# The Hadamard products of an FFN's weights, halved on GpSimd and moved among the last projections

## The chip, the cores and the metric

The kernel runs on one core of one Trainium2 chip. The metric is the device time of one execution in microseconds (us).

## The reference

The reference is one transformer block with adaptive layer norm, in float32. Input x is [2, 1024, 256]. From a conditioning vector come shifts, gains and gates for both halves of the block.

```python
h = layernorm(x) * (1 + ca) + sa
x = x + ga * attention(h)          # 16 query heads, 4 key/value heads of 128, causal, projection
h = layernorm(x) * (1 + cb) + sb
x = x + gb * ffn(h)

def ffn(x):                        # HIDDEN 256, INTER 1024
    x = fwht(x * SU_ug) / 64       # normalised Walsh-Hadamard transform
    x_up = x @ W_up.T * (Wscale_ug[:1024] * 64)
    x_gate = x @ W_gate.T * (Wscale_ug[1024:] * 64)
    x = silu(x_gate) * x_up
    x = fwht(x * SU_dp) / 64
    return x @ W_down.T * (Wscale_dp * 64)
```

A Hadamard transform of the activations is linear, so the kernel applies it to the weights instead, once.

## The kernel before

**Products.** A float32 matrix is split into a rounded high part (`_hi`, the type float32r) and a rest (`_lo`). A product is three matmuls: high by high, high by low, low by high (`three`, L1048 to L1050). So every operand of TensorE costs a rounding and a subtraction on other engines.

**Attention.** Eight turns `t` (two batches by four key/value heads). In a turn the eight row tiles `i` of queries are worked in four windows of two tiles, (7,0), (6,1), (5,2), (4,3). A window has nine units (i, j): `T` transposes four heads' probabilities on TensorE (L1177), ScalarE evicts the high part pt_hi (L722), VectorE the rest pt_lo (L946), and two units later `V` multiplies by the values. The transposes go to a ring of two PSUM banks: T of unit n needs pt_lo of unit n-2. `S` are scores; VectorE takes the maximum, ScalarE the exponential, and GpSimd divides by the sum (`normalise`, L573 and L578). `Y` is the projection of a finished row tile, 12 matmuls; VectorE adds it to x (L956). For all this a list, `WALK`, is written out by `walk()`, and each engine goes through it in order and issues its own part. T3 is below the transpose step of unit 3 of the last window of the last turn, V4 the value step of unit 4.

**The weights of the FFN.** They are six pieces of [128, 2, 512]: 0 to 3 are up and gate, 4 and 5 down. Each piece is multiplied by a Hadamard matrix of 256 (the down weights by one of 1024: two butterfly stages `B` on GpSimd, L543 to L549, and the same product). The 256 x 256 matrix is [[H, H], [H, -H]] with H of 128 x 128; in `weights(n)` both halves of the input are multiplied by H or -H and added in PSUM: 2 outputs k x 2 sources x (high, low) = 8 matmuls of 512 columns (L1224, L1225). The order of the pieces is `PIECES = [0, 1, 4, 5, 2, 3]`; n counts in that order. Around a product: `raw_high(n)` rounds the loaded piece (GpSimd, L615; for n = 1 ScalarE, L733), `raw_low(n)` subtracts (VectorE, L965; for n = 0 GpSimd, L621), `weights_high(n)` and `weights_low(n)` scale by SU, round and subtract the result (ScalarE L741, L746; VectorE L974, L979). The rounded input of n has two sets of buffers, in w_hi, w_lo and in o_hi, o_lo; W[n] are the two PSUM banks of its result.

**The FFN's first chunk.** The FFN works on four chunks of 512 rows. For tile m of the inner dimension `G` is gate and up (24 matmuls, `gate_up`), ScalarE makes the Silu (L754), VectorE the product g32 (L989), its rounding g_hi (L992) and the rest g_lo (L994), and `D` multiplies by the down weights (12 matmuls, `down`). In the first chunk these steps are mixed with the pieces (`P`) and the layer norm of the second batch (`L`), in an order written by hand, the list `FIRST`. The later chunks are a loop. D0 is the down step of tile 0, P2 the product n = 2, G0 the gate and up step of tile 0.

Of the kernel before, what the change touches and what calls it, by code (L numbers as in the profile page):

```python
# [73 lines left out]
def walk():  # L74
# [15 lines left out]
    for t in range(TURNS):  # L90
# [16 lines left out]
        for p, pair in enumerate(WINDOWS):  # L107
# [21 lines left out]
            if t + 1 == TURNS and p > 1:  # L129
                fill[2].append((t, "B", p - 2, 0))  # L130
# [13 lines left out]
    return out + [(TURNS - 1, "Y", i, 0) for i in WINDOWS[-1][::-1]]  # L144
# [25 lines left out]
def build(nc, x_in, wqkv, wv, wproj, wmod, c_cols, wug, wdn, su_ug, su_dp, ws_ug, ws_dp, ident_in, mask_in, had_in, out):  # L170
    ctx = ExitStack()
    with ctx:
# [462 lines left out]
        def _(act):  # L635
# [99 lines left out]
            def weights_high(n):  # L735

                piece = PIECES[n]
                for k in range(KH):
                    act.wait_ge(fmm_s, n * KH + k + 1)
                    if piece < 4:  # L740
                        a_.activation(wu_hi[:, k, piece * CH:(piece + 1) * CH], W[n][k], ACT.Identity,  # L741
                                      scale=su_u[:, k:k + 1]).then_inc(fhi_s, 1)
                    else:
                        for one in range(2):
                            m = 2 * (piece - 4) + one
                            last = a_.activation(wd_hi[k][:, m, :], W[n][k][:, one * HID:(one + 1) * HID],  # L746
# [578 lines left out]
```

## Time and profile before

| | us |
|---|---|
| median of 3 runs | 947.99 (946.07 to 948.47) |
| the profiled execution | 945.94 |
| its span in the profile | 944.0 |
| TensorE busy | 921.1 |
| VectorE busy | 641.0 |
| ScalarE busy | 501.2 |
| GpSimd busy | 459.4 |

The rows below are of the one profiled execution; the time that was measured for it is 1.9 us longer than its span, and the median of the runs is 2.05 us above it. Times in the trace count from the start of the span. PE is TensorE, PEld its loading of weights, DVE VectorE, ACT ScalarE, POOL GpSimd, SPq the queue that issues DMAs. The attention takes up the span to about 787 us, the FFN's weights and first chunk to about 840, the other three chunks the rest.

### The profile page before, as it was taken

What the parts mean: (1) busy time and instruction counts of PE and PEld (TensorE: products, weight loads), DVE (VectorE), ACT (ScalarE), POOL (GpSimd) and SP (SyncE); (2) the same over time, 40 slices, a digit from 0 to 9 for tenths busy, and PEclk for the clock granted to TensorE, in tenths of its full rate; (3) what the DMA queues carried; (4) which work ended last, traced back from release to release, by engine and by line L of the source; (5) the groups of instructions that cost most, each with busy time, mean ns of one, the idle gap of its engine ahead of it and who ended that gap; (6) DMA issues with size and microseconds to landing.
All of it is one profiled execution on the core that took longest, in us unless ns stands there. A gap on an engine that the chain in (4) does not pass through costs nothing.

```text
span 944.0 us, 14992 instructions
## 1 busy us (share of the span) xinstructions
PE 921.1 (98%) x5536; PEld 814.0 (86%) x5536; DVE 641.0 (68%) x1312; ACT 501.2 (53%) x1062; POOL 459.4 (49%) x655
## 2 busy tenths in 40 slices
PE   5989999999999999999999999999999999999997
PEld 4878889888888898888888888888888887888886
DVE  6567667865887577647875777478757876864554
ACT  3376556654665466547664766476647665321111
POOL 2375727670767185707671767076717684120000
PEclk9999999999999999999999999999999999999999
DMA  7000100000001000000010000000001011000000
GB/s 278 23 1 1 40 1 23 1 28 1 23 2 40 1 23 1 29 1 23 1 40 1 24 1 30 1 24 1 1 1 46 1 56 46 1 19 5 22 22 22
DMA packets 10179, 21.33 MB, mean 23 GB/s; under 512 B 1280, under 2 KB 5632, under 8 KB 9984
## 3 DMA queue, kind: packets, MB, share of 16 engines
q1 hardware_dynamic: 9392, 20.24, 6.2%
q8 instruction: 41, 0.67, 0.3%
q10 hardware_dynamic: 720, 0.21, 0.1%
q14 instruction: 26, 0.21, 0.1%
HBM read 18.35 MB, written 2.10 MB: 22 GB/s over the span
## 4 chain that ended last, share of the span: by engine, by line
PE 80%; DVE 11%; ACT 6%; issue 2%; DMA 1%; SPq 0%; DVEq 0%; POOL 0%; ACTq 0%
PE ps L1048 18%; PE ps L1050 17%; PE ps L1049 17%; PE ps L1177 10%; PE ps L1166 5%; PE ps L1160 5%; PE ps L1163 5%; DVE ps L942 4%; ACT prob L697 3%; DVE pt_lo L946 2%; ACT pt_hi L722 2%; DVE xhat L820 1%; PE ps L1072 1%; DVE stats L804 1%; DMA w_raw<-in_wqkv 1%
## 5 line engine op out<-in xcount | busy, mean ns | idle before, releaser
L573 POOL TENSOR_TENSOR rinv<-rsum,mone 128x1 f32<-128x1 f32 x256 | 141.4, 552 | 252.9 <-ACT prob L697 252.9
L946 DVE TENSOR_TENSOR pt_lo<-ps,pt_hi 128x512 fp32r<-128x512 f32 x288 | 198.3, 689 | 63.0 <-ACT pt_hi L722 59.9
L722 ACT ACTIVATE pt_hi<-ps 128x512 fp32r<-128x512 f32 x288 | 170.8, 596 | 123.8 <-PE ps L1177 123.5
L697 ACT ACTIVATE prob<-ps,nmax 128x128 f32<-128x128 f32 (+25 forms) x256 | 181.8, 710 | 85.5 <-DVE nmax L942 84.5
L942 DVE CUSTOM_DVE_ANT_0 ps<-ps,mask_f 128x128 f32<-128x128 f32 (+25 forms) x256 | 184.4, 726 | 46.2 <-PE ps L1166 44.1
L578 POOL TENSOR_SCALAR prob<-prob,rinv 128x128 f32<-128x128 f32 (+25 forms) x256 | 187.5, 733 | 43.2 <-POOL rinv L573 43.2
L1177 PE MATMUL ps<-ident,prob 128*128 128x128 f32 x1152 | 172.0, 273 | 1.6 <-POOL prob L578 1.2
L1177 PEld LDWEIGHTS ps<-ident,prob 128*128 128x128 f32 x1152 | 140.5, 140 | 19.9 <-DVE pt_lo L946 2.0
L1048 PE MATMUL ps<-pt_hi,v_hi 128*128 128x512 f32 x288 | 134.2, 466 | 0.0
L1050 PE MATMUL ps<-pt_hi,v_lo 128*128 128x512 f32 x288 | 113.7, 395 | 0.0
L1049 PE MATMUL ps<-pt_lo,v_hi 128*128 128x512 f32 x288 | 113.5, 394 | 0.0
L1160 PE MATMUL ps<-k_hi,q_hi 128*128 128x256 f32 (+16 forms) x384 | 108.3, 336 | 2.7 <-ACT prob L697 2.0
L1166 PE MATMUL ps<-k_hi,q_lo 128*128 128x256 f32 (+16 forms) x384 | 106.7, 332 | 0.0
L1163 PE MATMUL ps<-k_lo,q_hi 128*128 128x256 f32 (+16 forms) x384 | 106.5, 331 | 0.0
L1160 PEld LDWEIGHTS ps<-k_hi,q_hi 128*128 128x128 f32 x384 | 68.8, 189 | 18.3 <-ACT prob L697 7.2
L898 DVE SCALAR_TENSOR_TENSOR q_lo<-ps,q_hi 128x512 fp32r<-128x512 f32 x64 | 44.0, 691 | 53.9 <-ACT q_hi L686 53.9
L686 ACT ACTIVATE q_hi<-ps 128x512 fp32r<-128x512 f32 x64 | 38.3, 599 | 74.5 <-PE ps L1050 74.5
L1163 PEld LDWEIGHTS ps<-k_lo,q_hi 128*128 128x128 f32 x384 | 69.7, 188 | 6.2
L754 ACT ACTIVATE prob<-ps,ws_u 128x512 f32<-128x512 f32 x32 | 22.0, 687 | 97.2 <-PE ps L1050 97.2
L1048 PE MATMUL ps<-wp_hi,o_hi 128*128 128x256 f32 x256 | 73.1, 286 | 0.0
L1166 PEld LDWEIGHTS ps<-k_hi,q_lo 128*128 128x128 f32 x384 | 69.7, 188 | 3.2
L1050 PE MATMUL ps<-wp_hi,o_lo 128*128 128x256 f32 x256 | 72.4, 283 | 0.0
(145 smaller groups left out, 1785.2 us busy)
## 6 DMA issues: line engine op xcount, KB each, us to landing
w_raw<-in_wqkv SPq DMA_DIRECT2D x8, 640.0 KB, 3.9
wp_raw<-in_wproj SPq DMA_DIRECT2D x8, 512.0 KB, 3.4
prob<-in_wug SPq DMA_DIRECT2D x4, 512.0 KB, 5.1
out_y<-prob SPq DMA_DIRECT2D x8, 256.0 KB, 2.2
x<-in_x SPq DMA_DIRECT2D x3, 512.0 KB, 12.7
prob<-in_wmod SPq DMA_DIRECT2D x1, 1024.0 KB, 10.1
wv_raw<-in_wv SPq DMA_DIRECT2D x4, 256.0 KB, 4.9
raw_down<-in_wdn SPq DMA_DIRECT2D x1, 1024.0 KB, 4.7
```

The lines of the kernel that those rows point to most:

```text
L578: g_.tensor_scalar(row(i, h), row(i, h), rinv[:, at, h:h + 1], 1.0, ALU.mult, ALU.mult).then_inc(prob_done, 1)
L697: a_.activation(row(i, h).rearrange("p (a n) -> p a n", a=nb), score_banks(i, h).rearrange("p (a n) -> p a n", a=nb)[:, :, 0:w], ACT.Exp, ...
L722: a_.activation(pt_hi[:, n % 3, :], ring(t, "T", n), ACT.Copy).then_inc(pth_done, 1)
L942: v_.tensor_tensor_reduce(scores, scores, late, -1.0, 3.0e38, ALU.add, ALU.min, nmax[:, place(n), h:h + 1]).then_inc(max_done, 1)
L946: v_.tensor_tensor(pt_lo[:, n % 3, :], ring(t, "T", n), pt_hi[:, n % 3, :].bitcast(F32), ALU.subtract).then_inc(ptl_done, 1)
L1048: mm(dst, w_h, r_h, start=start, stop=False)
L1049: mm(dst, w_h, r_l, start=False, stop=False)
L1050: return mm(dst, w_l, r_h, start=False, stop=stop)
L1160: mm(dst[:, a * CH:a * CH + wide], queries(q_hi, n, h), k_hi[:, a * w:a * w + wide], start=True, stop=False)
L1163: mm(dst[:, a * CH:a * CH + wide], queries(q_hi, n, h), k_lo[:, a * w:a * w + wide], start=False, stop=False)
L1166: last = mm(dst[:, a * CH:a * CH + wide], queries(q_lo, n, h), k_hi[:, a * w:a * w + wide], start=False, stop=True)
L1177: last = tr(ring(t, "T", n)[:, q * P:(q + 1) * P], row(i, q, j * P, (j + 1) * P), ident[:, :])
```

## The change

- The 256-wide product is done as a sum and a difference, H(a + b) and H(a - b), of a piece's two halves. GpSimd forms a + b and a - b for each of the six pieces (`last_butterfly`), two operations of 128x512, and a product is then 2 outputs x (high, low) = 4 matmuls. The matrices -H are gone.
- The butterflies `B` of the down weights stand earlier in `WALK`: the first at the end of window (6,1), which puts it before GpSimd's normalisations of tile 4, the second after the first score step of tile 3.
- The pieces n = 0 and 1 are worked within `WALK`: ScalarE rounds them (`RH`) ahead of its evictions of units 4 and 6 of the last window, GpSimd subtracts, and the products P0 and P1 stand behind the two last projections. n = 1 has the key buffers for its halves and PSUM banks S[1] for its result. Piece 0 is loaded to w_raw, earlier.
- For n = 2 to 5 GpSimd adds, subtracts and rounds, in halves, and VectorE subtracts the low part in halves.
- In the first chunk ScalarE rounds g_hi (`gated_high`) in place of VectorE.

```diff
-            if t + 1 == TURNS and p > 1:
-                fill[2].append((t, "B", p - 2, 0))
+            if t + 1 == TURNS and p in (1, 2):
+                fill[8 if p == 1 else 4].append((t, "B", p - 1, 0))
+            if t + 1 == TURNS and p == 3:
+                for n in range(2):
+                    fill[4 + 2 * n].append((t, "RH", n, 0))
...
-    return out + [(TURNS - 1, "Y", i, 0) for i in WINDOWS[-1][::-1]]
+    for n, i in enumerate(WINDOWS[-1][::-1]):
+        out += [(TURNS - 1, "Y", i, 0), (TURNS - 1, "P", n, 0)]
+    return out
...
-FIRST = [("P", 0), ("P", 1), ("G", 0), ("P", 2), ("G", 1), ("D", 0), ("P", 3), ("G", 2), ("D", 1), ("P", 4), ("G", 3),
+FIRST = [("G", 0), ("P", 2), ("G", 1), ("D", 0), ("P", 3), ("G", 2), ("D", 1), ("P", 4), ("G", 3),
...
+        def halves_of(piece):
+            return raw_sum[sum_slot(piece)], raw[piece][:, 1, :]
...
-        W = [X if n == 1 else T for n in range(len(PIECES))]
+        W = [[S[1][:, 0:CH], S[1][:, CH:2 * CH]] if n == 1 else T for n in range(len(PIECES))]
...
             sp.dma_start(raw_down[:, :], wdn).then_inc(raw_s[4], 16)
+            sp.dma_start(raw[0], wug[0, :, :].rearrange("p (k n) -> p k n", k=KH)).then_inc(raw_s[0], 16)
...
-            for n in range(4):
+            for n in range(1, 4):
...
+            def last_butterfly(n):
+                a, b = raw[n][:, 0, :], raw[n][:, 1, :]
+                pool.wait_ge(fly_s, 2)
+                if n < 4:
+                    pool.wait_ge(raw_s[n], 16)
+                g_.tensor_tensor(raw_sum[sum_slot(n)], a, b, ALU.add)
+                g_.tensor_tensor(b, a, b, ALU.subtract).then_inc(last_fly_s, 1)
...
-            pool.wait_ge(raw_s[0], 16)
-            raw_high(0)
-            pool.wait_ge(rhi_s, 1)
-            g_.tensor_tensor(raw_lo[0], raw[0], raw_hi[0].bitcast(F32), ALU.subtract).then_inc(rlo0_s, 1)
-            pool.wait_ge(fly_s, 2)
+            for n in range(2):
+                last_butterfly(PIECES[n])
+            for n in range(2):
+                pool.wait_ge(rhi_s, n + 1)
+                for k, z in enumerate(halves_of(PIECES[n])):
+                    last = g_.tensor_tensor(raw_lo[n][:, k, :], z, raw_hi[n][:, k, :].bitcast(F32), ALU.subtract)
+                last.then_inc(rlo01_s, 1)
             for n in range(2, len(PIECES)):
-                if PIECES[n] < 4:
-                    pool.wait_ge(raw_s[PIECES[n]], 16)
-                raw_high(n)
+                last_butterfly(PIECES[n])
+                pool.wait_ge(fmm_s, (n - 1) * KH)
+                if n == 3:
+                    pool.wait_ge(y_done, (TURNS + 1) * NT)
+                pool.wait_ge(last_fly_s, n + 1)
+                for k, z in enumerate(halves_of(PIECES[n])):
+                    last = g_.tensor_scalar(raw_hi[n][:, k, :], z, 1.0, 1.0, ALU.mult, ALU.mult)
+                last.then_inc(rhi_s, 1)
...
+                if what == "RH":
+                    act.wait_ge(last_fly_s, n + 1)
+                    if n == 1:
+                        act.wait_ge(s_done, this(s_done, t, 32))
+                    for k, z in enumerate(halves_of(PIECES[n])):
+                        last = a_.activation(raw_hi[n][:, k, :], z, ACT.Copy)
+                    last.then_inc(rhi_s, 1)
+                if what == "P":
+                    weights_high(n)
...
-            act.wait_ge(raw_s[1], 16)
-            act.wait_ge(y_done, (TURNS + 1) * NT)
-            a_.activation(raw_hi[1], raw[1], ACT.Copy).then_inc(rhi1_s, 1)
...
+            def gated_high(m):
+                act.wait_ge(g32_s, m + 3)
+                a_.activation(g_hi[:, g_slot(m), :], g32[:, m % 2, :], ACT.Copy).then_inc(ghi_s, 1)
...
                 if what == "G":
                     gate(0, n)
+                    gated_high(n)
...
+                if what == "P":
+                    weights_low(n)
+                    if n == 1:
+                        raw_low(2)
...
-                gated(0, n)
+                gated(0, n, False)
...
-                plus, minus = mats[:, 0:P], mats[:, P:2 * P]
-                for k in range(KH):
-                    for src in (0, 1):
-                        mat = minus if k and src else plus
-                        mm(W[n][k], mat, raw_hi[n % 2][:, src, :], start=not src, stop=False)
-                        last = mm(W[n][k], mat, raw_lo[n % 2][:, src, :], start=False, stop=bool(src))
-                    last.then_inc(fmm_s, 1)
+                mat = had_r[PIECES[n] // 4]
+                for k in range(KH):
+                    mm(W[n][k], mat, raw_hi[n][:, k, :], start=True, stop=False)
+                    mm(W[n][k], mat, raw_lo[n][:, k, :], start=False, stop=True).then_inc(fmm_s, 1)
...
+                    if n == 1:
+                        pe.wait_ge(wf_ok, KH * 2)
```

## Rows read from the trace of the kernel before

**Rows 1.** The page: busy time of the engines, and the chain by engine.

```profile
PE 921.1 (98%) x5536; PEld 814.0 (86%) x5536; DVE 641.0 (68%) x1312; ACT 501.2 (53%) x1062; POOL 459.4 (49%) x655
...
PE 80%; DVE 11%; ACT 6%; issue 2%; DMA 1%; SPq 0%; DVEq 0%; POOL 0%; ACTq 0%
```

**Rows 2.** Busy time by stretches: engines, granted clock, DMA share, GB/s.

```profile
787.50:798.00 10.50, 9.87 (x53) 7.95 (x52) 6.71 (x9) 5.79 (x8) 2.36 (x2) 1.00 0.22 81
798.00:823.00 25.00, 24.94 (x134) 21.32 (x134) 20.61 (x42) 9.56 (x17) 3.83 (x4) 1.00 0.00 1
```

**Rows 3.** Timeline of TensorE: start, duration, line, out<-in, count, idle before.

```profile
777.61 0.60 PE L1177 MATMUL ps<-ident,prob 128*128 128x128 f32 x4
...
782.43 0.60 PE L1177 MATMUL ps<-ident,prob 128*128 128x128 f32 x4
...
787.50 0.29 PE L1048 MATMUL ps<-wp_hi,o_hi 128*128 128x256 f32 x1
...
790.62 0.40 PE L1224 MATMUL ps<-w_hi,had_r 128*128 128x512 f32 x1
790.85 0.40 PE L1225 MATMUL ps<-w_lo,had_r 128*128 128x512 f32 x1
...
793.25 0.50 PE L1224 MATMUL ps<-o_hi,had_r 128*128 128x512 f32 x1 [0.63 <-DVE o_lo L965]
...
795.21 0.40 PE L1048 MATMUL ps<-h_hi,q_hi 128*128 128x512 f32 x1
...
798.16 0.47 PE L1224 MATMUL ps<-w_hi,had_r 128*128 128x512 f32 x1
...
820.93 0.38 PE L1048 MATMUL ps<-k_hi,pt_hi 128*128 128x256 f32 x1
```

**Rows 4.** Timeline of GpSimd.

```profile
745.59 0.88 POOL L578 TENSOR_SCALAR prob<-prob,rinv 128x736 f32<-128x736 f32 x1 [0.21 <-POOL rinv L573]
...
755.60 1.28 POOL L512 TENSOR_TENSOR h_lo<-h,h_hi 128x512 fp32r<-128x512 f32 x1
...
764.41 2.40 POOL L543 TENSOR_TENSOR sum_down<-raw_down 128x1024 f32<-128x1024 f32 x1
...
769.12 0.55 POOL L573 TENSOR_TENSOR rinv<-rsum,mone 128x1 f32<-128x1 f32 x1
...
776.40 1.29 POOL L548 TENSOR_TENSOR raw_down<-sum_down 128x512 f32<-128x512 f32 x1
...
781.41 1.05 POOL L615 TENSOR_SCALAR w_hi<-prob 128x1024 fp32r<-128x1024 f32 x1
...
800.41 1.36 POOL L615 TENSOR_SCALAR w_hi<-prob 128x1024 fp32r<-128x1024 f32 x1 [3.91 <-PE ps L1225]
```

**Rows 5.** Timeline of the DMA queue SP.

```profile
772.27 0.33 SPq L478 DMA_DIRECT2D prob<-in_had  x1
```

**Rows 6.** Timeline of ScalarE.

```profile
716.64 1.16 ACT L672 ACTIVATE v_hi<-raw_down 128x512 fp32r<-128x512 f32 x2
...
780.79 0.60 ACT L722 ACTIVATE pt_hi<-ps 128x512 fp32r<-128x512 f32 x1 [1.96 <-PE ps L1177]
...
788.32 1.28 ACT L730 ACT_TABLE_LOAD   x1
```

**Rows 7.** Timeline of VectorE in the first chunk.

```profile
799.71 0.43 DVE L992 CAST pt_hi<-prob 128x512 fp32r<-128x512 f32 x1
800.17 0.69 DVE L994 TENSOR_TENSOR pt_lo<-prob,pt_hi 128x512 fp32r<-128x512 f32 x1
...
814.80 0.75 DVE L804 BATCH_NORM_STATS2 stats<-x 128x6 f32<-128x256 f32 x2
...
818.95 0.74 DVE L989 SCALAR_TENSOR_TENSOR prob<-ps,ws_u,prob 128x512 f32<-128x512 f32 x1
```

**Rows 8.** Timeline of VectorE: the same pair of operations at two times.

```profile
745.89 1.05 DVE L820 TENSOR_SCALAR xhat<-x,mv,rstd 128x256 f32<-128x256 f32 x2
...
817.04 0.73 DVE L820 TENSOR_SCALAR xhat<-x,mv,rstd 128x256 f32<-128x256 f32 x2 [0.90 <-POOL rstd L505]
```

More of the change, by code:

```diff
@@ L242, in build @@
         guard_a, guard_b = sum_dn[:, 0, :, :], sum_dn[:, 1, :, :]
-        had_f = prob[:, 0, 0, 0:CH].rearrange("p (a n) -> p a n", a=2)
-        raw = [prob[:, n // 2, n % 2 * 2:n % 2 * 2 + 2, CH:2 * CH] for n in range(4)]
+        had_f = prob[:, 0, 0, 0:2 * P].rearrange("p (a n) -> p a n", a=2)
+        raw = [w_raw[:, :, 0:CH] if n == 0 else prob[:, n // 2, n % 2 * 2:n % 2 * 2 + 2, CH:2 * CH] for n in range(4)]
         raw += [raw_down[:, n * KH * CH:(n + 1) * KH * CH].rearrange("p (k n) -> p k n", k=KH) for n in range(2)]
@@ L686, in chunk, with weights_high @@
                     a_.activation(query_chunk(q_hi, h, half), by_squares(bank(t, c)), ACT.Copy, scale=SCALE).then_inc(qkv_hi, 1)
+            def weights_high(n):
+                piece = PIECES[n]
+                for k in range(KH):
+                    act.wait_ge(fmm_s, n * KH + k + 1)
+                    if piece < 4:
+                        a_.activation(wu_hi[:, k, piece * CH:(piece + 1) * CH], W[n][k], ACT.Identity,
+                                      scale=su_u[:, k:k + 1]).then_inc(fhi_s, 1)
+                    else:
+                        for one in range(2):
+                            m = 2 * (piece - 4) + one
+                            last = a_.activation(wd_hi[k][:, m, :], W[n][k][:, one * HID:(one + 1) * HID],
+                                                 ACT.Identity, scale=su_d[:, 4 * k + m:4 * k + m + 1])
+                        last.then_inc(fhi_s, 1)
             waiting = []
@@ L730, in _ @@
             a_.activation(sc[:, 1, :, :], sc[:, 0, :, :], ACT.Silu)
-            act.wait_ge(raw_s[1], 16)
-            act.wait_ge(y_done, (TURNS + 1) * NT)
-            a_.activation(raw_hi[1], raw[1], ACT.Copy).then_inc(rhi1_s, 1)
-            def weights_high(n):
-                piece = PIECES[n]
-                for k in range(KH):
[L739 to L746, printed above, removed]
-                                                 ACT.Identity, scale=su_d[:, 4 * k + m:4 * k + m + 1])
-                        last.then_inc(fhi_s, 1)
             def gate(c, m):
@@ L905, in v_low, with raw_low, weights_low @@
                                      v_hi[:, 4 * n:4 * n + 4, :].bitcast(F32), ALU.subtract).then_inc(v_lo_s, 1)
+            def raw_low(n):
+                dve.wait_ge(rhi_s, n + 1)
+                for k, z in enumerate(halves_of(PIECES[n])):
+                    last = v_.tensor_tensor(raw_lo[n][:, k, :], z, raw_hi[n][:, k, :].bitcast(F32), ALU.subtract)
+                last.then_inc(rlo_s, 1)
+            def weights_low(n):
+                piece = PIECES[n]
+                for k in range(KH):
+                    dve.wait_ge(fhi_s, n * KH + k + 1)
+                    if piece < 4:
+                        at = slice(piece * CH, (piece + 1) * CH)
+                        v_.scalar_tensor_tensor(wu_lo[:, k, at], W[n][k], su_u[:, k:k + 1], wu_hi[:, k, at].bitcast(F32),
+                                                ALU.mult, ALU.subtract).then_inc(wf_ok, 1)
+                    else:
+                        for one in range(2):
+                            m = 2 * (piece - 4) + one
+                            last = v_.scalar_tensor_tensor(wd_lo[k][:, m, :], W[n][k][:, one * HID:(one + 1) * HID],
+                                                           su_d[:, 4 * k + m:4 * k + m + 1], wd_hi[k][:, m, :].bitcast(F32),
+                                                           ALU.mult, ALU.subtract)
+                        last.then_inc(wf_ok, 1)
             for t, what, n, h in WALK:
@@ L991, in gated @@
                 dve.wait_ge(g32_s, c * NM + m + 3)
[L992 removed]
+                if split:
+                    v_.tensor_copy(g_hi[:, g_slot(m), :], g32[:, m % 2, :]).then_inc(ghi_s, 1)
                 dve.wait_ge(ghi_s, c * NM + m + 1)
@@ L1132, in chunk, with weights @@
                 last.then_inc(qkv_done, 1)
+            def weights(n):
+                if n == 0:
+                    pe.wait_ge(ptl_done, (TURNS + 1) * NU)
+                    pe.wait_ge(consts, 1)
+                if n == 1:
+                    pe.wait_ge(exp_done, this(exp_done, TURNS - 1, 32))
+                if n < 2:
+                    pe.wait_ge(rlo01_s, n + 1)
+                else:
+                    pe.wait_ge(rlo_s, n - 1)
+                    pe.wait_ge(wf_ok, KH * n)
+                mat = had_r[PIECES[n] // 4]
+                for k in range(KH):
+                    mm(W[n][k], mat, raw_hi[n][:, k, :], start=True, stop=False)
+                    mm(W[n][k], mat, raw_lo[n][:, k, :], start=False, stop=True).then_inc(fmm_s, 1)
             for t, what, n, h in WALK:
@@ L1303 @@
         had = np.block([[had, had], [had, -had]])
-    had = np.concatenate([s * had / n ** 0.5 for n in (HID, INTER) for s in (1, -1)], axis=1).astype(np.float32)
+    had = np.concatenate([had / n ** 0.5 for n in (HID, INTER)], axis=1).astype(np.float32)
     arrays = {
```

57 lines of the change are left out of this document (13 added, 44 removed).

## The prediction

> **What bounds the kernel now.** I read the page first: TensorE is busy 98% of the span, and the chain that ended last lies 80% on it [rows 1]. Anything else matters only where it makes TensorE wait or work. The table of stretches then shows the place of the change, the hand-over from the last attention window to the FFN: TensorE is busy 9.87 of 10.50 us there and 24.94 of 25.00 in the stretch behind, at a granted clock of 1.00 (the level of 2.4 GHz) [rows 2]. So two things can be won: matmuls, and some 0.6 us of idle time. In the matmul timeline [rows 3] see the order of the steps named above: T3 777.61, T6 782.43, first Y 787.50, P0 790.62, P1 793.25, G0 795.21, P2 798.16, D3 820.93. The one start with idle time printed is P1: 0.63 us, for a VectorE subtraction.
>
> **Less TensorE work.** The 512-column matmuls of a piece start 0.23 us apart [rows 3]. A piece has 8 of them before and 4 after: six pieces save 24 x 0.232 = 5.6 us of TensorE time. If TensorE stayed the only limit, that and the idle time would be the whole gain. The sums and differences go to GpSimd, and all that follows is about who becomes late instead.
>
> **GpSimd and the last window.** The second butterfly stage is four operations of 128x512, from 776.40 to 781.41 [rows 4]: 1.25 us each, so a piece's sum and difference cost 2.5 us. GpSimd works in program order, and both stages move ahead: the first (764.41 to 769.12, 4.7 us) now stands before the four normalisations of row tile 4, the second (5.0) before the last three of tile 3. A normalisation costs 1.46 (five from 769.12 to 776.40 [rows 4]). From the end of h_lo at 755.60 + 1.28 = 756.9: stage one to 761.6, five normalisations to 768.9, stage two to 773.9, three more to 778.3. Before, the last was done at 776.4. The transposes T3 start at 777.61 [rows 3], the fourth needs the last normalisation 0.33 later: T3 stalls about 0.4 us.
> Then the first pair runs 778.3 to 780.85, the second to 783.4 (the DMA of its raw piece is the first behind the load issued at 772.27 [rows 5], so in time; the other raw piece comes before the window). ScalarE's rounding of piece 0 stands in front of its eviction of unit 4, which began at 780.79 [rows 6]. ScalarE is in order, so this eviction, VectorE's pt_lo and V4 queue behind GpSimd. Two 128x512 copies from SBUF take 1.16 us [rows 6]: 780.9 to 782.0, eviction (0.60) to 782.65, pt_lo (0.69, the form of g_lo [rows 7]) to 783.4. T6 needs that buffer and was at 782.43: +1.0. Rounding piece 1 waits for the second pair: 783.4 to 784.6, eviction of unit 6 and pt_lo to 785.95; T8, two units of 1.13 behind T6, was at 784.69: +1.3. The last window ends 1.3 us later; the 0.4 of T3 is inside that.
> GpSimd then makes the low halves of pieces 0 and 1, to 786.0 and 788.5 (2 x 1.25 each), before P0 and P1 need them (790 and 792). The copies of the Hadamard matrices halve, which VectorE's waits hide.
>
> **The hand-over.** The first Y starts at 787.50 + 1.3 = 788.8. Y 1.44 (12 matmuls of 0.12), P0 0.93 (4 x 0.232), Y 1.44, P1 0.93 put G0 at 793.55, against 795.21: -1.65. P0 fills the time in which the second Y waited, and P1's halves are ready. The Silu table load (1.28 [rows 6]) moves behind the evictions of P1, to about 794.6 to 795.9; G0's first Silu can begin at 796.5, which hides it by 0.6 us.
>
> **From G0 to D3: VectorE and ScalarE.** TensorE's own work there is 5 G x 2.73 + 4 P x 0.93 + 3 D x 1.44 = 21.7 us; before it was 25.72 (820.93 - 795.21), with P at 1.86. But VectorE's chain was nearly full: its g32 of tile 3 began only at 818.95, behind a layer norm begun at 814.80 [rows 7], and D3 waited for it. What the change does to that chain: the cast of g_hi (0.43, next start 0.46 later [rows 7]) goes to ScalarE, but VectorE is in order and waits for it, and one copy of 128x512 there is 0.60 to 0.64 with the hand-over (half of 1.16, and the fill [rows 6]): +0.18 each. And ScalarE now rounds g before it evicts the piece behind it. A round with a down piece: g32 0.79, wait 0.64, g_lo 0.60, wait for the piece's first eviction 0.24, two subtractions 0.79, 0.12 more of waiting, 0.79, raw_low in two halves 1.21: 5.18 us. With an up piece 4.66. So G0's start + 2.73 + 0.26 + 0.72 (Silu) = 3.7; two rounds 10.35; one of 4.66; layer norm 4.15 (814.80 to 818.95); the last round up to g_lo 2.2. Together 25.1 us against 25.7: only 0.6 of the 3.7 us saved on P2 to P5 survive. It shows as idle time of TensorE: about 1 us before D0, about 2 before D3. I add 0.3 for small gaps that such a sum leaves out. Without anything else D3 is 1.65 + 0.6 - 0.3 = 2.0 us earlier. Behind D3 a G, D and L take 4.6 us and VectorE 4 to 4.5, and the later chunks are untouched: the shift stays.
>
> **Contention, the unknown term.** The rows show GpSimd and VectorE holding each other up when both work from SBUF. VectorE's two xhat that began 0.3 us inside a GpSimd scaling of 0.88 us took 1.05 against 0.73 alone [rows 4, 8]; GpSimd's rounding that began inside VectorE's g_lo of 800.17 took 1.36 against 1.05 [rows 4, 7]. After the change GpSimd is busy about 90% of the time from 788.5 to 804 (four times 2.5 + 1.2), and in that time VectorE has six subtractions with both inputs in SBUF (raw_low of pieces 4 and 5 in halves, g_lo of tiles 0 and 1), all on its full chain. Lower bound: nothing. Upper bound: each waits for a whole sum, 1.0 us, 6 us in all. Between them: an op that comes at a random point waits some 0.6 less the 0.2 that the xhat row shows to be free before the end, times six, some 2.4; a part falls into VectorE's waits for ScalarE (0.36 a round). I take 1.3.
> The Trainium skill (SBUF — State Buffer, Who interferes with whom) says that a VectorE instruction with two SBUF inputs contends with a GpSimd one that reads SBUF, and that the loser blocks until the other is through. The xhat and rounding rows agree in direction; that it holds for a VectorE subtraction behind a GpSimd sum no row here shows. What it gives is rival 2.
>
> **Sum.** Profiled execution: 945.94 (span 944.0 and 1.9 around it) - 2.0 + 1.3 = 945.2. The median of the runs is 947.99, 2.05 above the profiled one; the same difference gives 947.3, a gain of 0.07%. A measurement of this kernel tells about 0.3% (2.8 us) from no change.
>
> **Rivals.**
> 1. TensorE keeps its saving. If ScalarE and VectorE had slack that I don't see, the gain is 5.6 + 0.9 of idle time - 1.3 (last window) = 5.2: 942.8. Against it: D3 already waited for VectorE. The partial form (no contention, and no stall in the last window because GpSimd is through sooner) is 2.0 + 1.3 = 3.3: 944.7. Chance of a gain over 2.8: 0.15.
> 2. Slower: VectorE held by GpSimd. If the six subtractions wait a full 1.0 us each and the two casts of the Hadamard matrices, in front of pt_lo of unit 5, 0.5 each, the term is 7 and the result -2.0 + 7 = +5: 953. It decides from a mean wait of 0.8 us on (six times 0.8 = 4.8, less 2.0). GpSimd's sums back to back speak for it; that the xhat pair lost only 0.3 speaks against. Chance 0.13.
> 3. No contention on the path: -2.0, 946.0. Chance 0.22, inside "same".
> 4. My case, 947.3, between 946.3 and 950.5: 0.50.
>
> **How the numbers follow.** Cases 3 and 4 are "same", 0.72; faster 0.15; slower 0.13. The range goes from the partial form of rival 1 (944.9) to a contention term of 4.6 (950.6).
>
> **What would show it.** Right: four matmuls a piece; T3, T6 and T8 late by 0.4, 1.0, 1.3; G0 at 793.5; idle time of 1 us before D0 and of 2 us before D3, both released by VectorE; raw_low and g_lo longer than 0.69 us while GpSimd adds. Wrong: D3 without idle time (rival 1), subtractions of 1.5 us and more (rival 2), or the transposes of units 4 to 8 on their old spacing of 1.13 us.

## The result, and the profile after

| us | before | after |
|---|---|---|
| median of 18 runs each, on the same chips | 946.21 (945.85 to 948.48) | 948.33 (946.49 to 951.06) |
| the profiled execution | 945.94 | 950.35 |
| its span | 944.0 | 948.4 |

The ratio of the times is 1.0018, with a 95% interval of 1.001 to 1.0025: slower by about 1.7 us, where a gain of 0.07% was forecast. The times of each kernel lie on levels some 2 us apart, so medians and means differ: the medians stand 2.1 us apart, the means (946.75 and 948.53) 1.8. The loss is 1.7 to 2.1 us.

The 18 runs of after don't scatter evenly. Each has its mean granted clock beside it:

| runs of after | us | mean granted clock |
|---|---|---|
| 6 | 946.49 to 947.42 | 0.998 to 0.999 |
| 7 | 948.10 to 949.53 | 0.998 |
| 5, the profiled one among them | 950.20 to 951.06 | 0.994 |

That turns out to be half of the story.

First the page of after, its busy times and its chain by engine, against [rows 1]:

```profile
PE 920.6 (97%) x5512; PEld 813.0 (86%) x5512; DVE 640.4 (68%) x1307; ACT 506.4 (53%) x1073; POOL 478.8 (50%) x673
...
PE 74%; DVE 13%; ACT 6%; POOL 3%; issue 2%; DMA 0%; DVEq 0%; SPq 0%; POOLq 0%; ACTq 0%
```

The 24 matmuls are gone (5536 to 5512), but TensorE is busy only 0.5 us less, not 5.6. Its share of the chain fell from 80 to 74%, and GpSimd, absent before, holds 3%. So 5.1 us of matmul time came back (the two falls of the clock below are in it), and TensorE's idle time grew by 4.9 us, from 22.9 to 27.8 of the span. Now the stretches, with the columns of [rows 2]; the first is early in the attention, the last four follow each other behind it:

```profile
48.00:60.00 12.00, 9.55 (x39) 7.66 (x38) 6.69 (x18) 7.07 (x20) 8.99 (x14) 0.73 0.01 2
787.50:798.00 10.50, 10.48 (x61) 8.81 (x61) 6.79 (x12) 5.87 (x9) 9.18 (x10) 1.00 0.30 100
798.00:823.00 25.00, 20.86 (x105) 16.68 (x103) 20.53 (x37) 9.93 (x21) 11.94 (x12) 1.00 0.01 1
822.00:824.00 2.00, 0.17 (x1) 0.18 (x2) 1.23 (x3) 1.65 (x3) 0.44 (x1) 1.00 0.00 0
824.00:826.00 2.00, 2.00 (x14) 2.00 (x15) 1.75 (x3) 0.93 (x3) 0.00 (x0) 0.71 0.00 0
826.00:828.00 2.00, 2.00 (x8) 1.71 (x7) 1.39 (x4) 1.44 (x3) 0.00 (x0) 0.50 0.06 12
828.00:830.00 2.00, 2.00 (x10) 1.60 (x9) 1.59 (x6) 0.00 (x0) 1.45 (x2) 0.93 0.00 0
```

Three things stand here. In the first chunk (798 to 823) TensorE is idle for 4.1 of 25 us, which was 0.06. GpSimd works 9.18 of the 10.5 us of the hand-over, which was 2.36. And the granted clock falls twice. It is 0.73 in 48 to 60, long before anything that the change touches (1.00 in the profile of before). That fall comes in single executions of both kernels: of 33 runs of before beside experiment 1, four have a mean clock of 0.996 and lie at 948.14 to 948.63, some 2 us above the others' middle of 946.4. No trace of such a run of before was taken, but of the thirteen profiles here seven show the early fall (0.72 to 0.86 in 48 to 60 us), and all seven are of executions on the upper level of their kernel (948.61 against 946.2 to 946.6 in experiment 1, 945.97 against 944.2 to 944.6 in experiment 3); the other six show 1.00. In after's profile the clock falls again to 0.50, the level of 1.2 GHz, right after TensorE was nearly idle (0.17 of 2.00 us). That one belongs to the change.

Because of that early fall I compare by marks inside the last window, in us from its first transposes. T, Y, G, P, D and L are the steps named above; L1, the layer norm step behind D4, is the mark for what follows D3 (D3, L0, G5, D4, L1).

| | T6 | T8 | Y | G0 | P2 | D0 | P3 | D3 | L1 |
|---|---|---|---|---|---|---|---|---|---|
| before | 9.66 | 11.92 | 14.73 | 22.44 | 25.39 | 30.04 | 31.48 | 48.16 | 54.32 |
| after | 10.45 | 13.68 | 16.50 | 21.21 | 24.75 | 29.85 | 32.82 | 49.00 | 56.74 |
| after minus before | +0.79 | +1.76 | +1.77 | -1.23 | -0.64 | -0.19 | +1.34 | +0.84 | +2.42 |

G0 is 1.2 us sooner; by D3 that and 0.8 more are gone; between D3 and L1 another 1.6. The timeline of TensorE shows where it stood (columns of [rows 3]):

```profile
785.28 0.66 PE L1232 MATMUL ps<-ident,prob 128*128 128x128 f32 x4 [0.20 <-DVE pt_lo L1011]
...
787.31 0.66 PE L1232 MATMUL ps<-ident,prob 128*128 128x128 f32 x4 [0.68 <-DVE pt_lo L1011]
...
799.58 0.50 PE L1186 MATMUL ps<-w_hi,had_r 128*128 128x512 f32 x1 [0.66 <-DVE w_lo L948]
...
804.68 0.39 PE L1086 MATMUL ps<-k_hi,pt_hi 128*128 128x256 f32 x1 [1.14 <-DVE v_lo L963]
...
807.65 0.50 PE L1186 MATMUL ps<-o_hi,had_r 128*128 128x512 f32 x1 [1.29 <-DVE o_lo L948]
...
823.83 0.38 PE L1086 MATMUL ps<-k_hi,pt_hi 128*128 128x256 f32 x1 [1.87 <-DVE pt_lo L1032]
```

The two T rows are T6 and T7. P2, D0, P3 and D3 wait 0.66, 1.14, 1.29 and 1.87 us, together 5.0, each for a VectorE instruction. D0 and D3 were forecast (1 and 2 us); P2 and P3 were not. VectorE in that stretch, against [rows 7]:

```profile
785.14 1.52 DVE L984 CAST had_r<-prob 128x128 fp32r<-128x128 f32 x2
...
797.82 0.68 DVE L948 TENSOR_TENSOR w_lo<-sum_down,w_hi 128x512 fp32r<-128x512 f32 x1
798.42 1.10 DVE L948 TENSOR_TENSOR w_lo<-raw_down,w_hi 128x512 fp32r<-128x512 f32 x1
...
801.26 1.80 DVE L1032 TENSOR_TENSOR pt_lo<-prob,pt_hi 128x512 fp32r<-128x512 f32 x1 [0.77 <-ACT pt_hi L791]
...
804.55 1.36 DVE L948 TENSOR_TENSOR o_lo<-sum_down,o_hi 128x512 fp32r<-128x512 f32 x1
805.84 1.76 DVE L948 TENSOR_TENSOR o_lo<-raw_down,o_hi 128x512 fp32r<-128x512 f32 x1
...
809.03 1.07 DVE L1032 TENSOR_TENSOR pt_lo<-prob,pt_hi 128x512 fp32r<-128x512 f32 x1 [0.77 <-ACT pt_hi L791]
...
823.08 0.69 DVE L1032 TENSOR_TENSOR pt_lo<-prob,pt_hi 128x512 fp32r<-128x512 f32 x1 [0.77 <-ACT pt_hi L791]
```

And GpSimd, in the form of [rows 4], with the last normalisations left out:

```profile
780.28 1.30 POOL L575 TENSOR_TENSOR dif_down<-w_raw 128x512 f32<-128x512 f32 x1
...
797.85 1.13 POOL L651 TENSOR_SCALAR o_hi<-sum_down 128x512 fp32r<-128x512 f32 x1 [0.19 <-POOL raw_down L576]
798.95 1.05 POOL L651 TENSOR_SCALAR o_hi<-raw_down 128x512 fp32r<-128x512 f32 x1
799.97 1.29 POOL L575 TENSOR_TENSOR dif_down<-prob 128x512 f32<-128x512 f32 x1
801.23 1.28 POOL L576 TENSOR_TENSOR prob<-prob 128x512 f32<-128x512 f32 x1
...
804.09 1.28 POOL L575 TENSOR_TENSOR dif_down<-prob 128x512 f32<-128x512 f32 x1
805.33 1.73 POOL L576 TENSOR_TENSOR prob<-prob 128x512 f32<-128x512 f32 x1
808.94 0.62 POOL L651 TENSOR_SCALAR o_hi<-dif_down 128x512 fp32r<-128x512 f32 x1 [1.89 <-PE ps L1187]
```

Put the two side by side. g_lo of tile 0 begins at 801.26, 0.03 us inside the GpSimd difference of 801.23. That ends at 802.51, g_lo at 803.06: it takes 1.80 where the same form takes 0.69 at 823.08, with GpSimd quiet. The same sum for all five that are stretched:

| VectorE subtraction begins | GpSimd instruction that it meets ends | subtraction ends | behind it by |
|---|---|---|---|
| 798.42 | 797.85 + 1.13 = 798.98 | 799.52 | 0.54 |
| 801.26 | 801.23 + 1.28 = 802.51 | 803.06 | 0.55 |
| 804.55 | 804.09 + 1.28 = 805.37 | 805.91 | 0.54 |
| 805.84 | 805.33 + 1.73 = 807.06 | 807.60 | 0.54 |
| 809.03 | 808.94 + 0.62 = 809.56 | 810.10 | 0.54 |

Whatever the meeting, a sum or a rounding, early in it or late, the subtraction ends 0.54 us behind the other's end. It doesn't run slower, it stands: of its 0.68 us only 0.14 pass beside the other. The same holds in all the traces of the experiments: 39 subtractions of this form that begin inside a GpSimd instruction, in eleven kernels, end 0.52 to 0.56 us behind it. Over 0.68 alone the five lose 0.42 + 1.12 + 0.68 + 1.08 + 0.39 = 3.7 us. It goes both ways: the GpSimd difference of 805.33 met the o_lo of 804.55, and took 1.73 against 1.28. The two casts of the Hadamard matrices, in front of the pt_lo that T7 waits for, take 1.52 together at 785.14, beside GpSimd's difference of piece 1 and low half of piece 0.

### The profile page after: what moved, and what is told of

The parts are those of the page before. It is cut to its first block, busy times and chain, and to the rows that moved or that the text cites. A ratio compares the mean times of both kernels' runs of the same rounds, so it can differ in the third digit from the quotient of the medians.

```text
span 948.4 us, 14983 instructions
## 1 busy us (share of the span) xinstructions
PE 920.6 (97%) x5512; PEld 813.0 (86%) x5512; DVE 640.4 (68%) x1307; ACT 506.4 (53%) x1073; POOL 478.8 (50%) x673
## 2 busy tenths in 40 slices
DMA packets 10180, 21.21 MB, mean 22 GB/s; under 512 B 1280, under 2 KB 5760, under 8 KB 9984
## 4 chain that ended last, share of the span: by engine, by line
PE 74%; DVE 13%; ACT 6%; POOL 3%; issue 2%; DMA 0%; DVEq 0%; SPq 0%; POOLq 0%; ACTq 0%
PE ps L1086 17%; PE ps L1088 16%; PE ps L1087 16%; PE ps L1232 9%; PE ps L1215 5%; PE ps L1218 5%; PE ps L1221 5%; DVE ps L1007 4%; ACT prob L738 3%; DVE pt_lo L1011 2%; ACT pt_hi L763 2%; DVE xhat L857 1%; PE ps L1110 1%; DVE stats L841 1%; POOL prob L604 1%
## 5 line engine op out<-in xcount | busy, mean ns | idle before, releaser
L1087 PE MATMUL ps<-wp_lo,o_hi 128*128 128x256 f32 x256 | 72.1, 282 | 0.0
```

Source lines behind the costliest of these rows:

```text
L1087: mm(dst, w_h, r_l, start=False, stop=False)
```

## The experiments

Times are medians, with the ratio to runs of before taken beside them, and its 95% interval. After stands at 948.33, ratio 1.0018.

**1. g_hi back to VectorE.** After, without the part that gives the rounding to ScalarE:

```diff
-                    gated_high(n)
...
-                    gated(0, n, False)
+                    gated(0, n)
```

> The changed kernel, but VectorE rounds g_hi in the first chunk again. In the changed kernel's trace the way from g32's start to g_lo's start is 1.51 us (before: 1.25), four times ahead of D3, and ScalarE's evictions of the down pieces wait behind the rounding. Theory 'the hop to ScalarE is a main cost': D3 comes 1.0 to 1.5 us sooner after G0 (27.8 us now), median down by 1 us or more. Rival 'VectorE is held by GpSimd': the cast is one more VectorE operation from SBUF, is itself held by GpSimd in tiles 0 and 1, and D3 gains under 0.5 us.

Measured: 946.55, ratio 1.0002 (0.9993 to 1.0011). D3 is at 48.20, 0.8 sooner than after, less than the 1.0 to 1.5 expected: in tile 0 the cast on VectorE is itself held by GpSimd (1.01 us in place of 0.43). In the idle time before it, and in the clock behind it, the profile differs too:

```profile
823.65 0.38 PE L1085 MATMUL ps<-k_hi,pt_hi 128*128 128x256 f32 x1 [1.15 <-DVE pt_lo L1031]
```

```profile
824.00:826.00 2.00, 2.00 (x18) 1.96 (x17) 1.97 (x4) 0.12 (x1) 0.00 (x0) 1.00 0.00 0
826.00:828.00 2.00, 2.00 (x11) 1.64 (x10) 1.97 (x6) 0.90 (x2) 0.17 (x1) 1.00 0.03 8
```

1.15 us of idle time instead of 1.87, and the clock stays at 1.00 (2.4 GHz). Of the 1.5 us (by the ratios) to 1.8 us (by the medians) recovered, 0.8 is the position of D3; the rest is this, as I read it. The hop to ScalarE costs the chain 0.27 a tile, since g_lo starts 1.52 us after g32 begins (799.74 to 801.26) where it was 1.25 (798.92 to 800.17); I had 0.18.

**2. More matmuls in the idle time.** After, with the first six matmuls of G4, the G in front of D3, done twice (1.37 us more work):

```diff
-                for a in (0, 1):
+                for a in ((0, 0, 1) if twice else (0, 1)):
...
-                    gate_up(0, n)
+                    gate_up(0, n, n == 4)
```

> The changed kernel, with the first six matmuls of G4 done twice (1.37 us more TensorE work, inside the 2.5 us in which TensorE waits for D3's input; the result is the same). Theory 'the granted clock falls after the idle time before D3 and costs 1.6 us': the clock stays at 1.00 from 824 to 830 in the trace, D3 to L1 takes 6.2 us instead of 7.7, the median falls by 0.8 to 1.6 and the spread of the runs shrinks. Rival 'all of the loss is waiting, the fall of the clock is harmless or independent of this idle time': no change in time.

Measured: 947.1, and all 11 runs lie within 946.97 to 947.23; ratio 1.0002 (0.9993 to 1.0011), 1.5 us better than after by the ratios, by more work. D3 starts at 48.99, after's 49.00, and waits 0.50 in place of 1.87. From D3 to L1 it takes 6.16 us, as before (after: 7.74), and the clock is full:

```profile
823.00:834.00 11.00, 11.00 (x71) 9.88 (x70) 8.30 (x23) 5.28 (x10) 3.98 (x4) 1.00 0.01 2
```

So the fall behind D3 follows the idle stretch in front of it and costs 1.6 us where it comes. It is the step between the first two groups of after's runs, and it is absent in all 11 here.

**3. No sums in the first chunk.** GpSimd adds and subtracts 2 of 512 columns, so the FFN's weights are not the reference's.

```diff
-                g_.tensor_tensor(raw_sum[sum_slot(n)], a, b, ALU.add)
-                g_.tensor_tensor(b, a, b, ALU.subtract).then_inc(last_fly_s, 1)
+                m = 512 if n < 2 else 2
+                g_.tensor_tensor(raw_sum[sum_slot(n)][:, 0:m], a[:, 0:m], b[:, 0:m], ALU.add)
+                g_.tensor_tensor(b[:, 0:m], a[:, 0:m], b[:, 0:m], ALU.subtract).then_inc(last_fly_s, 1)
```

> The changed kernel, but for the pieces n = 2 to 5 GpSimd's sum and difference cover 2 of 512 columns, so the FFN's weights are not the reference's; all else is as in the changed kernel. Theory 'VectorE is held by GpSimd's sums' (raw_low and g_lo took 3.7 us more than alone in the changed kernel's trace): the subtractions are back at 0.68 us each, D3 comes 2.5 to 3.7 us sooner after G0 than 27.8, and the clock stays up: median down by 3 to 5 us. Rival 'the hop to ScalarE and the order of the evictions set D3': G0 to D3 stays over 27.

Measured: 944.55, ratio 0.9979 (0.997 to 0.9988). D3 comes at 46.20: 2.8 sooner than after and 1.96 sooner than before. The same VectorE instructions as above, in this kernel:

```profile
797.80 0.68 DVE L949 TENSOR_TENSOR w_lo<-sum_down,w_hi 128x512 fp32r<-128x512 f32 x1
798.40 0.68 DVE L949 TENSOR_TENSOR w_lo<-raw_down,w_hi 128x512 fp32r<-128x512 f32 x1
...
801.24 0.93 DVE L1033 TENSOR_TENSOR pt_lo<-prob,pt_hi 128x512 fp32r<-128x512 f32 x1 [0.77 <-ACT pt_hi L792]
...
803.66 0.67 DVE L949 TENSOR_TENSOR o_lo<-sum_down,o_hi 128x512 fp32r<-128x512 f32 x1
804.26 0.68 DVE L949 TENSOR_TENSOR o_lo<-raw_down,o_hi 128x512 fp32r<-128x512 f32 x1
```

D0 to P3 is 1.53 us (2.97 in after), so the wait before P3 is all but gone. So the sums are what makes GpSimd hold the subtractions, and at D3 they cost 2.8 us. (Two of the five meetings above were with roundings; without the sums the roundings come earlier, o_hi's at 796.27 in place of 797.85.) The idle time before D3 is still 1.70 us, as forecast for a chain without contention, and the clock stays at 1.00 behind it.

**4. The roundings one unit later.** `RH` of pieces 0 and 1 stands ahead of units 5 and 7 in place of 4 and 6:

```diff
-                    fill[4 + 2 * n].append((t, "RH", n, 0))
+                    fill[5 + 2 * n].append((t, "RH", n, 0))
```

> The changed kernel, with ScalarE's two roundings one unit later in the last window (ahead of the evictions of units 5 and 7). Theory 'ScalarE waits for GpSimd's pairs and holds up its own evictions': the last window ends 0.7 to 1.3 us sooner (now 1.8 us late), GpSimd's low halves remain in time for P0 and P1, and the median falls by 0.7 to 1.3. Rival 'the casts of the Hadamard matrices, held 1.5 us by GpSimd in front of pt_lo of unit 5, set the loss': the last window stays 1.3 us late or more.

Measured: 948.85, ratio 1.0025 (1.0016 to 1.0034), which can't be told from after. T6 is 0.36 sooner, but T8 is where it was (13.70), because the casts now take 1.82 us there. My theory that the place of the rounding alone sets T8 fell: the casts take up what it gives. How much of T8's delay is theirs is read from experiment 6.

**5. The hop alone.** Before, with nothing but `gated_high` on ScalarE in place of VectorE's cast:

```diff
+                act.wait_ge(g32_s, m + 3)
+                a_.activation(g_hi[:, g_slot(m), :], g32[:, m % 2, :], ACT.Copy).then_inc(ghi_s, 1)
...
+                    gated_high(n)
...
-                    gated(0, n)
+                    gated(0, n, False)
```

> The kernel before, with one part of the change alone: in the first chunk ScalarE rounds g_hi in place of VectorE; products of eight matmuls, no sums, everything else as before. From the changed kernel's trace the way from g32's start to g_lo's start is 1.51 us against 1.25 with VectorE's own cast. Theory 'the hop costs, also without GpSimd's sums': four times 0.26 us ahead of D3, of which the gaps of the kernel before hide a part: D3 0.5 to 1.0 us later after G0 (25.7 before), median up by 0.5 to 1. Rival 'VectorE's gaps hide it, the hop costs only where VectorE is held by GpSimd': G0 to D3 within 0.3 of 25.7 and the time within 0.3.

Measured: 947.5, ratio 1.0011 (1.0002 to 1.0021). D0 is 0.82 later than before and D3 1.19, a little above the expectation. This part of the change loses 1.0 us by itself. Most of that is not the hop's own 0.27: it makes g_lo of tile 0 begin 0.04 us inside a GpSimd rounding that it preceded in before (800.17 against 800.41), and g_lo takes 1.55, 0.86 more than alone.

```profile
802.98 1.55 DVE L1001 TENSOR_TENSOR pt_lo<-prob,pt_hi 128x512 fp32r<-128x512 f32 x1 [0.77 <-ACT pt_hi L760]
```

```profile
802.94 1.05 POOL L615 TENSOR_SCALAR w_hi<-prob 128x1024 fp32r<-128x1024 f32 x1 [3.89 <-PE ps L1232]
```

**6. The Hadamard matrices cast sooner.** After, with `H` two units ahead:

```diff
-                fill[5].append((t, "H", 0, 0))
+                fill[3].append((t, "H", 0, 0))
```

> The changed kernel, with VectorE's two casts of the Hadamard matrices two units earlier in the last window (ahead of pt_lo of unit 3), where GpSimd runs short operations and not the pairs. In the changed kernel's trace the two casts took 1.52 us, for two 128x128, in front of pt_lo of unit 5, and T7 waited 0.7 us. Theory 'casts held by GpSimd': they take 0.5 us or less, T8 is at 13.0 or sooner after the window's first T (13.7 in the changed kernel, 11.9 before), the window ends 0.6 to 0.9 us sooner and the median falls by as much. Rival 'ScalarE's roundings alone set T8': T8 stays at 13.5 or later.

Measured: 947.25, ratio 1.0005 (0.9996 to 1.0014). The casts are held even longer, since GpSimd's sums run on through both:

```profile
780.71 2.35 DVE L984 CAST had_r<-prob 128x128 fp32r<-128x128 f32 x2
```

But VectorE has that time there: T8 is at 12.94 in place of 13.68, Y at 15.82 in place of 16.50 and D3 at 48.37 in place of 49.00. In after the casts' place costs the window 0.7 us; T8 is still 1.0 later than before without it.

This profile shows one thing more. D3 waits 1.87 us, to the hundredth what it waits in after, and the clock behind it does not fall; D3 to L1 takes 6.17 us:

```profile
823.35 0.39 PE L1086 MATMUL ps<-k_hi,pt_hi 128*128 128x256 f32 x1 [1.87 <-DVE pt_lo L1032]
```

```profile
824.00:826.00 2.00, 2.00 (x16) 1.90 (x16) 1.27 (x2) 0.93 (x3) 0.00 (x0) 1.00 0.03 8
```

So the 1.6 us are the clock's and not the idle time's, and an idle stretch of this length doesn't bring the fall every time.

**7. A version from these.** Edits 1 and 6, and VectorE's layer norm of the second batch spread over two rounds instead of standing in front of D3's g32:

```diff
                     if n == 4:
                         ln_front(2, 0, 0, 0)
+                    if n == 5:
                         ln_normalise(2, 0, 0, 0)
                         ln_front(2, 0, 1, 0)
```

> The changed kernel, with g_hi rounded by VectorE again, the casts of the Hadamard matrices two units earlier, and the second half of the layer norm's opening (normalise, next statistics) behind piece n = 5 and so behind g_lo of tile 3. Theory 'D3 is set by VectorE's chain, of which 2.8 us of layer norm stand ahead of it': idle time before D3 falls from 2.2 us to under 0.3, window end 0.7 sooner, G0 to D3 25.8 or less, the clock stays at 1.00, and the time is 944.0 to 945.3 (2 us under the kernel before at the most). Rival 'the layer norm is then late for L0 and D4': L0 or D4 waits 1 to 2 us and the time is that of the kernel before.

Measured: 944.24, ratio 0.9975 (0.9966 to 0.9984). D3 starts at 46.27 without idle time, and D3 to L1 is 6.07 us. Experiment 6 had D3 at 48.37 and the hop costs 0.8; I put the other 1.3 us down to the layer norm; it was not changed alone. What is left of the waits:

```profile
796.85 0.50 PE L1186 MATMUL ps<-w_hi,had_r 128*128 128x512 f32 x1 [0.66 <-DVE w_lo L947]
...
802.14 0.39 PE L1086 MATMUL ps<-k_hi,pt_hi 128*128 128x256 f32 x1 [1.37 <-DVE v_lo L962]
...
805.11 0.50 PE L1186 MATMUL ps<-o_hi,had_r 128*128 128x512 f32 x1 [1.29 <-DVE o_lo L947]
```

This one beats both kernels: 2.4 us under before by the ratio, and some 4 under after. Spreading the layer norm in the kernel before was not run; TensorE is busy 24.94 of 25.00 us there [rows 2], so I would expect little of it.

**8. A late D3 in the kernel before.** Six more `bn_stats` of a tile already in place, to a spare buffer, in front of the layer norm. It has nothing of the change, only its idle time:

```diff
+                        for i in range(6):
+                            v_.bn_stats(spare[:, i, :], x[:, NT, :])
```

> The kernel before, with six extra statistics operations (0.36 us each, results not used) on VectorE in front of the first layer norm statistics of the FFN, so that D3 waits 2.1 to 2.3 us; nothing else is changed. Theory 'idle time of TensorE before D3 lets the clock fall': a granted clock under 1.00 in the 8 us behind D3 in the profile or in a part of the runs, that is a second level 1.5 us above the first. Rival 'it takes the several waits of the changed kernel (before P2, D0, P3 and D3) together': the clock stays at 1.00, and the time is 2.2 us above the kernel before in all runs but for those with the other level that the kernel before has too.

Measured: 949.46, ratio 1.0026 (1.0016 to 1.0037). D3 waits 1.94 us and is 2.0 later than before; D3 to L1 is 7.73 us. TensorE, then the stretch behind it:

```profile
823.23 0.39 PE L1051 MATMUL ps<-k_hi,pt_hi 128*128 128x256 f32 x1 [1.94 <-DVE pt_lo L995]
```

```profile
824.00:828.00 4.00, 4.00 (x19) 3.73 (x19) 3.19 (x7) 1.02 (x2) 0.00 (x0) 0.61 0.02 4
```

There is one idle stretch here, not four as in after, so one of this length can be enough. Two of its eight runs lie at 948.0 with a mean clock of 1.00, the others at 949.3 to 950.2 with 0.996 to 0.998: the fall doesn't come in every execution. In how many of the six it came isn't shown, since the early fall can lift a run too, and one was traced.

**9. The first rounding later, the second behind the window.** The version of 7, with the first `RH` ahead of unit 5 and the second behind all evictions of the window:

```diff
-                for n in range(2):
-                    fill[4 + 2 * n].append((t, "RH", n, 0))
+                fill[5].append((t, "RH", 0, 0))
...
+            if len(behind) == 1 and t + 1 == TURNS:
+                out.append((t, "RH", 1, 0))
```

> The kernel of the best run so far (changed kernel, g_hi on VectorE, casts early, layer norm split), with ScalarE's two roundings placed where they wait least: of piece 0 ahead of the eviction of unit 5, of piece 1 behind the high half of the first finished tile, after all evictions. Theory 'ScalarE waiting for GpSimd's pairs is what is left of the last window's delay': first Y at 15.2 after the window's first T or sooner (15.83 now, 14.73 before), median 943.5 to 943.9. Rival 'GpSimd's low halves are then late for P0 and P1': the wait turns up there, and the time stays at 944.2 or rises.

Measured: 945.04, ratio 0.9983 (0.9974 to 0.9992), 0.8 above 7. The window does end 0.4 sooner. But GpSimd's low half of piece 1 now waits for ScalarE, and everything that GpSimd does later with it; GpSimd first, then P2:

```profile
790.43 1.30 POOL L643 TENSOR_TENSOR k_lo<-dif_down,k_hi 128x512 fp32r<-128x512 f32 x1 [2.60 <-ACT k_hi L771]
```

```profile
800.40 0.50 PE L1187 MATMUL ps<-w_hi,had_r 128*128 128x512 f32 x1 [2.60 <-DVE w_lo L948]
```

The sums met w_lo of P2 in place of others (1.77 and 1.74 us). Behind this wait the clock falls too, at another place than D3:

```profile
800.00:802.00 2.00, 1.60 (x5) 1.27 (x6) 1.93 (x4) 0.74 (x2) 2.00 (x3) 0.72 0.00 0
802.00:804.00 2.00, 2.00 (x6) 1.53 (x5) 2.00 (x3) 0.94 (x3) 2.00 (x2) 0.50 0.00 0
```

A miss: I had counted the window and not the queue behind it.

**10. Eight matmuls again for the two down pieces**, whose sums GpSimd then leaves out, on top of 9:

```diff
+                    if PIECES[n] > 3:
+                        for src in (0, 1):
+                            part_m = mat[:, P:2 * P] if k and src else mat[:, 0:P]
+                            mm(W[n][k], part_m, raw_hi[n][:, src, :], start=not src, stop=False)
+                            last = mm(W[n][k], part_m, raw_lo[n][:, src, :], start=False, stop=bool(src))
```

> As e9_best2, but the two down pieces (n = 2, 3) are multiplied as before the change, with eight matmuls and no sum and difference on GpSimd; the four up and gate pieces are halved. It costs 8 x 0.232 = 1.9 us of TensorE. Theory 'VectorE held by GpSimd's sums, in front of P2, D0 and P3 (0.66, 1.37 and 1.29 us of idle time), costs more than the halving of these two pieces saves': the three idle times shrink to 1 us or less in all, and the time is 0.5 to 1.4 us under e9_best2. Rival 'the idle times have other causes (order of evictions on ScalarE)': 1 to 1.9 us above e9_best2.

Measured: 945.71, ratio 0.9987 (0.9978 to 0.9996), 0.7 above 9. GpSimd started the sums of the up pieces sooner and held the same subtractions:

```profile
802.12 3.09 DVE L953 TENSOR_TENSOR o_lo<-raw_down,o_hi 128x512 fp32r<-128x512 f32 x2
```

The wait of P2 shrank from 2.60 to 2.15, but P3, which had none in 9, now waits 0.69, so TensorE's added 1.9 us bought nothing. The clock stays at 1.00 behind the 2.15. Another miss.

**11. The version of 7 without sums**, the edit of 3 on top of it, as a bound:

> The kernel of e7_best1 with GpSimd's sum and difference of the pieces n = 2 to 5 over 2 of 512 columns only (weights not the reference's). It bounds what the sums' hold on VectorE still costs there. Theory: idle time before P2, D0 and P3 falls from 3.3 to under 0.8 us, and the time from 944.2 to 941.5 to 942.5. Rival: the idle times stay over 2 us, so they come from VectorE's own load.

Measured: 942.07 (4 runs), ratio 0.9948 (0.9933 to 0.9963). P2 waits 0.24, D0 0.90, P3 next to nothing (D0 to P3 is 1.54), some 1.2 in all where under 0.8 was expected, and D3 is 2.4 sooner than in 7. Even in the best version the sums on GpSimd cost 2.2 to 2.4 us of VectorE's time on the path.

## Why the prediction was wrong

The shape was right: TensorE doesn't keep its saving, since VectorE's chain to D3 carries what GpSimd and ScalarE add. The sign came out otherwise, and the sum shows by which terms. At D3 I forecast -2.0 + 1.3 = -0.7 and it was +0.84; behind D3 I had nothing and it was +1.6 in the profile. The forecast time of 947.3 stands only 1.0 from the measured 948.33, and its range holds it, but by luck: the base was the median of three runs, 947.99, of which two lay on the upper level, and 18 runs put it at 946.21. From there my terms give 945.5, and the change of -0.7 was really +1.7 to 2.1.

- **Contention, "I take 1.3"**: the step that failed. It measured 2.8 at D3 (experiment 3), and 3.7 in the stretched instructions. My middle bound, 2.4, stood in the text: six meetings, each with 0.6 of the other's instruction to come, less 0.2 that is free. Five of the six met, with 0.56, 1.25, 0.82, 1.22 and 0.53 to come, 4.4 in all where 3.6 was reckoned, and each had 0.14 free and not 0.2. So the meetings were not at random points: my reading of the timelines is that the ends of the same products set off GpSimd's roundings and sums and VectorE's evictions, and one meeting lengthens the GpSimd instruction that the next one meets (the 1.73). From 2.4 I took off 1.1 for a part that would fall into VectorE's waits for ScalarE, 0.36 a round. Of the 3.7, 0.9 did not add to D3: 0.4 fell into the wait for the Silu ahead of g32 of tile 0, 0.2 into the round of tile 1, and 0.25 is g_lo's 0.93, which experiment 3 keeps. The round of tile 0, where most of it arose, had no wait left to take any: it is 2.64 us longer than in experiment 3 (g32 to g32, 7.78 against 5.14). By the Trainium skill (SBUF — State Buffer, Who interferes with whom) the loser blocks until the other is through; the five rows above agree, but for the 0.14. It was rival 2 in kind, at less than its price: the mean over the six subtractions is 3.7 / 6 = 0.6, and I had put the turning point at 0.8.
- **A term that wasn't there: the clock.** A forecast idle time of 2 us before D3 was priced as waiting alone. In most runs, going by their times, it also drops the granted clock to 0.50 behind it, for 1.6 us more (experiments 2, 6 and 8). The lesson is that I had the length of the stretch and did not ask what it does to the engine that stands.
- **The last window, 1.3**: measured 1.77. T3's last transpose was 0.4 late, as forecast. T6 was 0.79 late (forecast 1.0), T8 1.76 (1.3). The casts of the Hadamard matrices, put at nothing as hidden by VectorE's waits, took 1.52 us beside two GpSimd subtractions, in front of pt_lo of unit 5; sooner casts give back 0.7 (experiment 6). Only rival 2 priced them. The other 1.0 of T8's delay I put down to the roundings, for which 1.3 was forecast.
- **G0, -1.65**: -1.23, the difference being the window. Everything between went as reckoned: Y, P0, Y, P1 from 16.50 to 21.21 is 4.71 us, forecast 4.75. The Silu table load was hidden.
- **G0 to D3 without contention**, forecast 25.1 and 0.3: 25.0 in experiment 3, and D3 -1.96 against -2.0. VectorE's rounds came out at 5.14 and 5.10 (forecast 5.18), 4.65 (4.66), the layer norm at 4.14 (4.15). Inside the first two, errors cancel: the hop to ScalarE was 0.27 and not 0.18, g_lo of tile 0 took 0.93, and the 0.36 of waiting for ScalarE's evictions hardly came. The 0.3 for small gaps wasn't needed. That D3 itself agrees to 0.04 is luck: the window was 0.4 later than forecast, and G0 to D3 0.4 shorter.
- **Together**: window +0.4, contention +1.5, the rest -0.4 give +1.5 at D3, which is what was missed there; the clock adds 1.6 in 12 of 18 runs, going by their times. 0.84 + 1.6 x 12/18 is 1.9, beside a loss of 1.7 to 2.1.

The range's lower end is given as 944.9 and, for the same case, as 944.7; nothing hangs on it.

Left open: why the clock falls at 48 to 60 us in some executions of either kernel, and what decides in which; and why the later fall came behind idle stretches of 1.87 (after), 1.90, 1.94 and 2.60 us, and not behind 1.70, 1.87 (experiment 6) and 2.15. That the 7 runs in the middle are those with the late fall alone rests on their mean clock and on experiment 4, whose profiled execution (949.13) has 7.76 us from D3 to L1 and no early fall; the traces of those runs themselves weren't taken. That the same GpSimd work with VectorE's operands in another memory would hold nothing wasn't tried.

## What to carry to other kernels

Matmuls taken off a full TensorE are worth only what the engine that feeds the next product can follow; add up that engine's chain first, and move the work off its path too (here the layer norm, 1.3 us). Work given to GpSimd is not free for VectorE: two streams set off by the same event meet in every round, so look for each VectorE subtraction from SBUF that begins inside a GpSimd instruction, and let it end 0.54 us behind that. And a stall of about 2 us can have two prices, the wait and the slower clock behind it; where it can't be removed, filling it with repeated matmuls was cheaper here than standing (experiment 2).

## What the runs showed of the hardware

- A VectorE subtraction of 128x512 from SBUF takes 0.68 us alone, and ends 0.52 to 0.56 us behind the end of a GpSimd sum, difference or rounding that it begins in: 0.93 to 1.81 us here, 39 cases in eleven traces. A VectorE cast of 128x512, with one input (0.43 us alone), ends 0.28 to 0.29 us behind: 1.01 us in experiment 1. Two casts of 128x128 took 1.52 us (after) to 2.35 us (experiment 6) beside sums and subtractions, though they are small.
- After TensorE stood 1.87 (after), 1.90 (experiment 4) or 1.94 us (8) before D3 the granted clock fell to 0.50, and D3 to L1 took 7.7 in place of 6.2 us; after 2.60 us (9, before P2) it fell too. After 1.87 us in experiment 6, 2.15 in 10 and 1.70 in 3, and after 1.15 or 0.50, it stayed at 1.00. 1.37 us of repeated matmuls in the stall made the kernel 1.5 us faster, and its runs agreed within 0.26 us.
- The early fall (0.73 in 48 to 60 us against 1.00) goes with a second level some 2 us higher in the times: all seven profiles that show it (0.72 to 0.86) are of runs on that level, whatever was changed 700 us later.
